# Moving the transposes of an x tile next to a unit's transposes of probabilities in a fused LayerNorm and masked attention kernel

## What is computed

```
# x: (16, 1024, 512) f32; adj: (1024, 1024) of 0 and 1; W*: (512, 512); 8 heads of 64
h = jnp.maximum(_layernorm(x, axis=-1), 0.0)
q = (h @ Wq + bq).reshape(b, n, H, HD)      # k and v likewise
scores = jnp.einsum('bihd,bjhd->bhij', q, k) / jnp.sqrt(jnp.float32(HD))
mask = jnp.where(adj == 0, -1000000000.0, 0.0)
weights = jax.nn.softmax(scores + mask[None, None, :, :], axis=-1)
out = x + jnp.einsum('bhij,bjhd->bihd', weights, v).reshape(b, n, H * HD)
```

## Time and profile before

| | |
|---|---|
| median of 3 runs | 4008.99 us (4007.49 to 4008.99) |
| the profiled execution | 4008.32 us |
| its span from first to last instruction | 4006.4 us |
| granted TensorE clock, mean | 0.998 |
| PE / PEld busy | 3978.3 us (99%) / 3285.6 us (82%) |
| DVE / ACT / POOL busy | 3069.0 us (77%) / 3079.3 us (77%) / 1391.1 us (35%) |

### The profile page before, as it was taken

How to read it: one execution, slowest core, us unless ns; L and a number is a source line. 1 busy time by engine, 2 the same in 40 slices (tenths; PEclk the granted TensorE clock), 3 DMA queues, 4 the chain that set the end, 5 groups by cost and what they waited for, 6 DMA issues and landing times. The chain is left out here.

```text
span 4006.4 us, 64401 instructions
## 1 busy us (share of the span) xinstructions
PE 3978.3 (99%) x22016; PEld 3285.6 (82%) x22016; DVE 3069.0 (77%) x5130; ACT 3079.3 (77%) x5514; POOL 1391.1 (35%) x1404
## 2 busy tenths in 40 slices
PE   8999999999999999999999999999999999999998
PEld 6888888888888888888888888888888888888886
DVE  7877778777787877878777687786876868768686
ACT  5877868778687887868868688686886868868687
POOL 4333333343333333333333333333333333333322
PEclk9999999999999999999999999999999999999999
DMA  5232222322222322223223232232322313323121
GB/s 192 70 87 67 84 76 70 86 74 83 81 63 83 88 68 82 71 74 94 61 82 83 62 94 67 78 86 58 93 81 63 95 51 93 89 57 97 45 68 48
DMA packets 239954, 314.82 MB, mean 79 GB/s; under 512 B 16401, under 2 KB 147473, under 8 KB 231057
## 3 DMA queue, kind: packets, MB, share of 16 engines
q1 hardware_dynamic: 239632, 310.71, 27.3%
HBM read 172.23 MB, written 37.75 MB: 52 GB/s over the span
## 5 line engine op out<-in xcount | busy, mean ns | idle before, releaser
L906 DVE TENSOR_TENSOR pT<-T,pT 128x512 fp32r<-128x512 f32 x2048 | 1391.0, 688 | 733.3 <-ACT pT L709 714.4
L709 ACT CAST pT<-T 128x512 fp32r<-128x512 f32 x2048 | 1184.7, 590 | 626.5 <-PE T L567 542.3
L900 DVE CUSTOM_DVE_ANT_0 S<-S,mask 128x1024 f32<-128x1024 f32 x1024 | 1252.5, 1223 | 3.7 <-PE S L553 3.7
L567 PEld LDWEIGHTS T<-ident,probs 128*128 128x128 f32 x8192 | 1006.9, 140 | 277.1 <-DVE pT L906 41.6
L567 PE MATMUL T<-ident,probs 128*128 128x128 f32 x8192 | 1231.8, 273 | 1.0 <-ACT probs L728 0.4
L728 ACT ACTIVATE probs<-S,negmax 128x1024 f32<-128x1024 f32 x1024 | 1151.7, 1125 | 11.8 <-DVE negmax L900 8.6
L586 PE MATMUL O<-pT,vs 128*64 128x512 f32 x2048 | 961.7, 470 | 0.2 <-DVE pT L906 0.2
L579 PE MATMUL O<-pT,vs 128*128 128x512 f32 x2048 | 815.9, 398 | 0.0
L521 PE MATMUL misc<-hT,wqk 128*128 128x512 f32 x3036 | 779.2, 392 | 0.0
L521 PEld LDWEIGHTS misc<-hT,wqk 128*128 128x128 f32 x3036 | 565.5, 188 | 125.6
L417 POOL TENSOR_TENSOR outs<-outs,oT 64x512 f32<-64x512 f32 x256 | 333.3, 1302 | 579.7 <-DMA outs<-oT 573.5
(11 more groups left out here) (74 smaller groups left out, 3440.2 us busy)
## 6 DMA issues: line engine op xcount, KB each, us to landing
wqk<-wqk_split SPq DMA_DIRECT2D x63, 1024.0 KB, 7.2
xln<-in_x SPq DMA_DIRECT2D x240, 256.0 KB, 2.7
outs<-in_x SPq DMA_DIRECT2D x66, 512.0 KB, 4.9
kA<-kA SPq DMA_DIRECT2D x128, 256.0 KB, 3.2
kB<-kB SPq DMA_DIRECT2D x128, 256.0 KB, 3.8
outs<-oT SPq DMA_DIRECT2D x256, 128.0 KB, 3.3
out<-outs SPq DMA_DIRECT2D x64, 512.0 KB, 4.3
adj_in_sb<-in_adj SPq DMA_DIRECT2D x4, 1024.0 KB, 14.4
```

Of the source, the lines that this page charges most:

```text
L567: mm = pe.transpose(T[:, u % 2, i * P:(i + 1) * P], probs[:, (GB * g + i) % RING, j * P:(j + 1) * P], ident[:])
L709: act.copy(pT[:, u % PT, 0, :], T[:, u % 2, :]).then_inc(p_hi, 1)
L900: dve.tensor_tensor_reduce(S[:, s % 2, :], S[:, s % 2, :], mask[:, s % NB, :], 1.0, 3.0e38, ALU.add, ALU.min, negmax[:, s % RING:s % RING ...
L906: dve.tensor_tensor(pT[:, u % PT, 1, :], T[:, u % 2, :], pT[:, u % PT, 0, :].bitcast(F32), ALU.subtract).then_inc(p_lo, 1)
```

## The change

Of each of the eight `turn_h` in batches 0 to 14 (120 of them, 480 transposes), the place on PE changes: from the end of `fill` to directly behind `turn_probs` of the same slot, ahead of `contract_lo` and the scores. Waits, data and buffers are as before, and no instruction is added or taken away.

```
@@ fill
                 if u in QK_AT and not (last and QK_AT[u][0] == PAIRS - 1):
                     p, k = QK_AT[u]
                     project_qk(b, p + 1, k, 1)
-                if u in HT_AT and not last:
-                    turn_h(b + 1, HT_AT[u], before(b, u, False, last))
@@ body
                     if u >= LAG or not first:
                         contract_hi(*ended)
                     turn_probs(b, u)
+                    if u in HT_AT and not last:
+                        turn_h(b + 1, HT_AT[u], before(b, u, False, last))
                     if u >= LAG or not first:
                         contract_lo(*ended)
                     score_ahead(b, u, last)
```

## The result

The changed kernel takes 4019.24 us (median of 9 runs, 4018.74 to 4020.69) against 4008.36 us (median of 9 runs, 4007.14 to 4008.99): 10.9 us or 0.27% slower, ratio 1.0028, 95% interval 1.002 to 1.0037. The profiled execution has a span of 4018.8 us, 12.4 more than before; with 4020.69 us it is the longest of its nine. The clock is 0.998 in both.

The account below looks back on a forecast made before the run. PE, busy 3978.3 of 4006.4 us, was taken to set the time; 0.22 + 0.69 = 0.91 us a batch, 15 times, adds 13.7 us, giving 4022.4 us, range 4014 to 4027.

Parts of the forecast that it names:

- Pace of the matmuls: Merged transposes on PE, eight taking 0.43 + 0.36 us: 1.33 against 1.34 apart, difference called rounding and taken as 0.
- the six slots: The slots other than 77 and 96: the bank and tile are ready in time, so loss taken as 0.
- Slot 77: `turn_h` still waits for ACT's L743 to free the bank, now with L586 behind it: loss 0.22 us a batch.
- Slots 94 and 96: Slot 94's late scores delay `shift` and `h_low` on DVE, so slot 96's `turn_h` waits: loss 0.69 us a batch.
- I take 0.43: Delay of slot 94's `shift` on DVE, taken equal to that of the scores, reading 0.49 as signal and matmul's end.
- a lower bound, with 0.39 for the signal: `shift` starting at least 0.39 behind the last score: delay 0.33 instead of 0.43, loss 0.59 us at slot 96.
- Slot 98: Next user of the bank, `turn_out` behind `h_low` of slot 96: covered by 0.25 us, so no wait.
- The sum: 0.22 + 0.69 = 0.91 us a batch, 15 times: 13.7 us, which PE has no idle time to make good.
- The merge saves a switch: Rival: each of 120 merged groups on PE saves 0.085 us, 10.2 us in all; faster had chance 0.03.
- Slot 96 loses only today's shortfall: Rival: `h_low` is not later, so 0.22 + 0.26 = 0.48 us a batch, 7.2 us, 4015.5; chance 0.06.
- No change: Rival: existing waits, such as 41.6 us for `p_lo`, shrink by what PE comes later: 4009 us; chance 0.05.
- The clock: Rival: PE's clock falls, one slow stretch a batch costing about 3.4 us, 51 us in all, 4073; chance 0.02.

Follow-up runs that it names:

- h_low_first: The changed kernel, but on DVE the low part (L873) of slot 94's tile stands ahead of that slot's L900: 4012.87 us beside 4008.75 for the kernel before.
- only_96: Against the kernel before, only slot 96's x tile is turned early, slot 94's scores stay ahead of its tile: 4012.03 us beside 4008.35.

## Why the prediction came out as it did

- **Pace of the matmuls: right.** The merged groups read 0.43 and 0.36 us as forecast, and the six slots without a wait together cost nothing (4007.12 beside 4008.35). The 0.01 us between the sums 1.34 and 1.33 was no rounding, though: from `T` to `T` each of the six slots is 0.005 to 0.018 shorter in the changed kernel, 0.07 in a batch, 1.0 us in all.
- **Slot 77: right.** Forecast 0.22 us in a batch; the rows give 0.23, the mean of the 15 batches 0.22, the kernel with this slot alone 3.0 / 15 = 0.20.
- **Slots 94 and 96: the mechanism right, the size a little too large.** Forecast 0.69, the rows give 0.63, and so does every batch to 0.01. The step that was off is "I take 0.43" for the delay of `shift`. The 0.49 between the last score and L900 was not the signal's time: where L900 really waits, it starts 0.42 behind the last score (2220.78 to 2221.20). DVE's own queue had held it for the other 0.07, so L900 came 0.35 later against `T` and L500 stood 1.05 behind `T`, not 1.10. That case was in the prediction as a lower bound, with 0.39 for the signal. `h_low_first` and `only_96` show the two halves of this term: the release queued behind L900, and the shortfall of the release as it was.
- **Slot 98: right**, it stayed covered.
- **The sum.** 15 x (0.22 + 0.63) = 12.8 us, less the 1.0 of the six slots: 11.8, and 11.8 is also what the trace gives from the first slot's `T` to the last batch's. The forecast was 13.7; 0.9 of the difference is the delay of `shift`, 1.0 the gain that I had rounded to 0. The span grew by 12.4: the other 0.6 stands ahead of the first slot, which starts at 56.5 us instead of 55.9 in the profiled execution. The change doesn't touch that start-up, and the kernel with all but slots 77 and 96 early starts there too, with a span of 4006.4. The medians differ by 10.9; the nine runs of the changed kernel scatter over 2.0 us, and I haven't traced the 0.9 between trace and medians. The forecast time, 4022.4, is 3.2 above the measured one: 2.8 from the difference, the rest from a kernel before that was taken at 4008.7 and measured at 4008.36.
- **The rivals.** "The merge saves a switch" fell with the six slots: the saving is 0.01 us a group, not 0.085. "Slot 96 loses only today's shortfall" describes `only_96`, where the scores of slot 94 aren't moved, and not the change. "No change" fell: the new waits are paid in full in every batch. The clock stayed at 0.998, with 0.45 us as the longest new wait of a matmul. By the rule of the Trainium skill that I weighed ("TensorE: Matmul & The Clock Gate", Part 4), longer runs of transposes could have cost clock. This trace has 120 more runs of eight transposes, at the same mean clock of 0.998.

## What to carry to other kernels

PE is busy nearly all the time here, and moving work within its queue changed next to nothing by itself (six of the eight places); what counted was the wait that moves with it, and how much ready work was then queued behind that wait instead of ahead of it. Check each moved wait against the end of its releaser, and then ask whether the move also delays that releaser: here the transposes delayed the scores, the scores delayed L900, and the release of the bank stood behind L900. A single bank that serves one user after another, or a table from which another engine takes its places too, makes a move of one slot a move on several engines. And where one instruction starts close behind another, look whether its engine was idle before it: only then does the distance show what the signal takes.

## What the runs showed of the hardware

- A 512-column matmul behind transposes is recorded with a longer start-to-start time (0.31 us instead of 0.23), but the transposes ahead of it are recorded shorter by nearly the same: four transposes take 0.36 us in front of a matmul and 0.43 in front of more transposes. So in these traces the longer time is no cost of switching; what a merge of two groups saves is 0.01 us.
- Where L900 waits for the scores, it starts 0.42 to 0.44 us behind the start of the last one, and PE's first transpose 0.14 to 0.15 behind the end of the ACT or DVE instruction that frees its bank. Four transposes behind such a wait take 0.38 us instead of 0.36.
